# Attention head loop: the queries' cosine product on GpSimd instead of VectorE, and score tile 4 parted 320 + 320

## The reference

```python
q = jnp.einsum('bim,mhd->bhid', x, wq)          # 8 batches x 8 heads = 64 heads of 1024 x 128
k = jnp.einsum('bim,mhd->bhid', x, wk)
q = rope(q)                                     # [even*cos - odd*sin, even*sin + odd*cos]
k = rope(k)
s = jnp.einsum('bhid,bhjd->bhij', q, k) / D_HEAD
s = s - INFTY_APPROX * (i < j)                  # causal
p = jax.nn.softmax(s, axis=-1)
o = jnp.einsum('bhij,bhjd->bhid', p, v)
x = layernorm(x + jnp.einsum('bhid,hdm->bim', o, wo))
...                                             # then soft dispatch to 8 x 64 slots, gelu FFN, combine, layernorm
```

## Time and profile before

| | |
|---|---|
| time, three runs | 1764.21, 1767.45, 1772.24 us; median 1767.45 |
| the profiled execution | 1769.15 us, its span 1767.3 us |
| PE busy | 1694.9 us (96%) |
| DVE busy | 1431.5 us (81%) |
| ACT busy | 1237.6 us (70%) |
| POOL busy | 1134.0 us (64%) |
| q's cosine product on DVE (L616) | x64, 78.4 us, 1224 ns each |
| k's cosine product on POOL (L412) | x64, 153.0 us, 2390 ns each |

### The profile page before, as it was taken

How to read it: one execution, slowest core, us unless ns; L and a number is a source line. 1 busy time by engine, 2 the same in 40 slices (tenths; PEclk the granted TensorE clock), 3 DMA queues, 4 the chain that set the end, 5 groups by cost and what they waited for, 6 DMA issues and landing times. The chain is left out here.

```text
span 1767.3 us, 33370 instructions
## 1 busy us (share of the span) xinstructions
PE 1694.9 (96%) x10524; PEld 1481.7 (84%) x10524; DVE 1431.5 (81%) x2945; ACT 1237.6 (70%) x2361; POOL 1134.0 (64%) x684
## 2 busy tenths in 40 slices
PE   5999999999999999999999999999999997999996
PEld 4788888888888888888888888888888886889886
DVE  4888988897889888977898889879889887677764
ACT  3777777776777777767777777777777763665663
POOL 4566666665666656666666666666666654677775
PEclk9999999999999999999999999999999999999999
DMA  4222232223222322232223222322232323123212
GB/s 143 65 61 77 73 101 61 76 73 86 66 74 73 100 67 73 73 97 73 73 73 96 73 73 73 96 73 72 72 85 72 85 73 93 46 62 94 60 31 54
DMA packets 76518, 134.23 MB, mean 76 GB/s; under 512 B 19264, under 2 KB 45888, under 8 KB 76352
## 3 DMA queue, kind: packets, MB, share of 16 engines
q1 hardware_dynamic: 74880, 130.10, 27.7%
q10 hardware_dynamic: 1472, 2.10, 0.4%
HBM read 56.36 MB, written 8.70 MB: 37 GB/s over the span
## 5 line engine op out<-in xcount | busy, mean ns | idle before, releaser
L493 ACT ACTIVATE probs<-ps_slot,neg_max 128x640 f32<-128x640 f32 (+7 forms) x512 | 378.7, 741 | 121.1 <-DVE neg_max L600 111.7
L600 DVE CUSTOM_DVE_ANT_0 ps_slot<-ps_slot,causal 128x640 f32<-128x640 f32 (+7 forms) x512 | 386.8, 756 | 58.1 <-PE ps_slot L57 57.3
L816 PE MATMUL ps_turn<-ident,probs 128*128 128x128 f32 x2304 | 338.8, 277 | 19.8 <-DVE x_t L657 6.3
L426 POOL TENSOR_TENSOR q<-rot_q,q 128x1024 fp32r<-128x1024 f32 x64 | 153.9, 2404 | 245.0 <-ACT q L510 245.0
L816 PEld LDWEIGHTS ps_turn<-ident,probs 128*128 128x128 f32 x2304 | 257.7, 141 | 51.6 <-DVE x_t L657 8.0
L55 PE MATMUL ps_slot<-k,q 128*128 128x512 f32 (+3 forms) x768 | 285.0, 371 | 2.7 <-DVE rot_q L616 1.5
L57 PE MATMUL ps_slot<-k,q 128*128 128x512 f32 (+3 forms) x768 | 267.8, 349 | 0.0
L56 PE MATMUL ps_slot<-k,q 128*128 128x512 f32 (+3 forms) x768 | 267.1, 348 | 0.0
L418 POOL TENSOR_TENSOR swapped_q<-swapped_q,rope 128x1024 f32<-128x1024 f32 x64 | 170.8, 2669 | 77.0 <-DMA swapped_q<-unrot_q 76.9
L426 POOL TENSOR_TENSOR k<-rot_k,k 128x1024 fp32r<-128x1024 f32 x64 | 153.1, 2392 | 82.3 <-ACT k L510 79.8
L527 ACT ACTIVATE pt_split<-ps_turn 128x512 fp32r<-128x512 f32 x256 | 145.2, 595 | 61.8 <-PE ps_turn L816 61.8
(11 more groups left out here) (168 smaller groups left out, 4348.6 us busy)
## 6 DMA issues: line engine op xcount, KB each, us to landing
swapped_k<-unrot_k SPq DMA_DIRECT2D x128, 256.0 KB, 3.6
swapped_q<-unrot_q SPq DMA_DIRECT2D x128, 256.0 KB, 3.7
inv_b<-inv_rows SPq DMA_DIRECT2D x64, 512.0 KB, 5.0
x_rows<-in_L_attn_x SPq DMA_DIRECT2D x8, 512.0 KB, 5.2
y_t<-y_sum SPq DMA_DIRECT2D x8, 512.0 KB, 5.2
x_rows<-y_t SPq DMA_DIRECT2D x8, 512.0 KB, 3.9
unrot_q<-in_L_attn_x SPq DMA_DIRECT2D x8, 512.0 KB, 5.4
row_b<-r_rows SPq DMA_DIRECT2D x16, 256.0 KB, 3.5
```

Source lines behind the costliest of these rows:

```text
L426: pool.tensor_tensor(out[:, 1, :], rot[which][:, :], f32(out[:, 0, :]), ALU.subtract)\
L493: act.activation(probs_tile(t), score_tile(name, head, i), ACT.Exp, scale=-1.0, bias=neg_max[:, head.par, t:t + 1], accum_out=sums[:, head ...
L600: dve.tensor_tensor_reduce(tile, tile, causal[:, T - WIDTH[t]:T], -1.0, UNSEEN, ALU.add, ALU.min, neg_max[:, head.par, t:t + 1]).then_inc( ...
L816: last = pe.transpose(bank[:, at:at + P], probs_tile(t)[:, j * P:(j + 1) * P], ident[:, :])
```

## The change

The q cosine product leaves DVE's stream; POOL makes it, reading ACT's copy in SBUF, between its sine product for k and its sine product for q. With it the wait of PE before tile 7's scores changes from `cos_made[0]` to `raw_made[0]` (the copy), and SP waits for `cos_made[0]` once, near the end. The scores of tile 4 are placed 192 columns into their slot, so that the bank's border parts them into 320 and 320 columns. The first head is changed likewise.

```diff
+SLOT_OFFSET = {"s4": 192}
...
-            return slot(name, head)[:, i * BANK:i * BANK + WIDTH[t]]
+            at = i * BANK + SLOT_OFFSET.get(name, 0)
+            return slot(name, head)[:, at:at + WIDTH[t]]
...
-            def mul_cos_k(head):
+            def mul_cos(which, head):
                 if not head.live():
                     return
                 if head.step(-1).live():
-                    wait_apart(pool, lo_made[1], head.step(-1).made(), pool_ticks)
-                wait_apart(pool, raw_made[1], head.made(), pool_ticks)
-                pool.tensor_tensor(rot[1][:, :], unrot[1][:, :], kept.rope[:, 0, :], ALU.mult).then_inc(cos_made[1], 1)
+                    wait_apart(pool, lo_made[which], head.step(-1).made(), pool_ticks)
+                wait_apart(pool, raw_made[which], head.made(), pool_ticks)
+                pool.tensor_tensor(rot[which][:, :], unrot[which][:, :], kept.rope[:, 0, :], ALU.mult)\
+                    .then_inc(cos_made[which], 1)
...
                 before, after = head.step(-1), head.step(1)
-                mul_cos_k(after)
+                mul_cos(1, after)
                 mul_sin(1, after)
+                mul_cos(0, after)
                 mul_sin(0, after)
                 split_lo(1, after)
                 split_lo(0, after)
...
-            def mul_cos_q(head):
-                if not head.live():
-                    return
-                dve.wait_ge(raw_made[0], head.made())
-                if head.step(-1).live():
-                    dve.wait_ge(lo_made[0], head.step(-1).made())
-                dve.tensor_tensor(rot[0][:, :], slot("q", head), kept.rope[:, 0, :], ALU.mult).then_inc(cos_made[0], 1)
...
                 before, after = head.step(-1), head.step(1)
-                mul_cos_q(after)
                 invert(before)
...
-                    for c0 in range(0, WIDTH[t], BANK):
-                        cols = slice(c0, min(c0 + BANK, WIDTH[t]))
+                    room = BANK - SLOT_OFFSET.get(name, 0)
+                    for cols in (slice(0, min(room, WIDTH[t])), slice(room, WIDTH[t])):
+                        if cols.start >= cols.stop:
+                            continue
...
-                free_slot(cos_made[0], after)
+                free_slot(raw_made[0], after)
                 scores("s7", head)
```

More of the change, by code:

```diff
@@ L376, in step @@
                     sp.wait_ge(swap_landed[0], last * 32)
+                    sp.wait_ge(cos_made[0], last)
                     sp.dma_start(kept.x_row, x[0, :, :].rearrange("(t p) m -> p t m", p=P)).then_inc(ahead_landed, 16)
@@ L478, in _ @@
             pool.wait_ge(rope_landed, 32)
-            mul_cos_k(first)
+            mul_cos(1, first)
             mul_sin(1, first)
+            mul_cos(0, first)
             mul_sin(0, first)
@@ L754, in _ @@
             first = Head(0, 0, heads)
-            dve.wait_ge(rope_landed, 32)
-            mul_cos_q(first)
             dve.wait_ge(wvo_hi, 1)
@@ L873, in step @@
                 if head.live() and not before.live():
-                    pe.wait_ge(cos_made[0], head.made())
                     pe.wait_ge(raw_made[0], head.made())
```

## The result

The changed kernel takes **1785.27 us** (median of 6 runs, 1783.42 to 1786.93). The kernel before, run beside it, took 1767.45 (6 runs, 1764.21 to 1772.24). The ratio is 1.0096, with a 95% interval of 1.0079 to 1.0113: about one per cent slower. The forecast was 1785.0.

The account below looks back on a forecast made before the run. PE was taken to bound the kernel, level with DVE in heads with the long addition. Ordinary heads 4, other heads 3 and k's swap 10 made 17 us on 1769.15, 1.7 above the median: about 1785 us, range 1744 to 1804.

Parts of the forecast that it names:

- The shared pair and the chain: POOL instructions and DVE's two-SBUF-input additions exclude each other; sine k, cosine q, addition, sine q, low k, addition: 21.96 us a head.
- The hand-over between two POOL instructions: At k's addition, DVE gets SBUF access 0.14 us before POOL's recorded end, though POOL has its next instruction ready.
- The rival in which POOL isn't let go: POOL shuts DVE's addition for k out through q's cosine and sine products: 1.4 us more in 61 heads, near 1870; chance 0.13.
- L616 met nobody: DVE's old q cosine product, reading PSUM and SBUF, contended with no POOL instruction: its bare 1.22 us beside one.
- PE keeps the lead: Rival: DVE's addition for q precedes POOL's low part of k, or additions are hidden; 21.45 us a head, about 1743; chance 0.20.
- PE's 0.3 us buy nothing: PE's gain per head from tile 4's split and the removed tile 7 wait doesn't count, being outside the POOL-DVE sequence.
- The term of 4 + 3 us for ordinary and heavy heads: Attention loop: 52 ordinary heads lose 0.085 us each, 4 us; the nine others, six with the short addition, 3 us more.
- The term of 10 us for k's swap: q's swap, issued earlier, delays k's swap and POOL's sine product for k by x = 0.2 us in 52 heads.
- The rival with head 1's delay: k's swap late by 0.5 us or more: 1802, up to 1857 with head 1's 1.64; chance 0.07.
- The first head and the tail: POOL's added product in the first head, at most 2.4 us once, taken as 0; SP's added wait near the end stands behind finished work.

## Why the prediction was right, and where it was not

The time was right to 0.3 us. Taken apart, the mechanism holds, and one of its three terms doesn't.

- **The shared pair and the chain: right.** Start of the sine product of k to start of the sine product of q: 4.70 us (expected 4.72, from +2.98 to +7.70). Both additions in the long form in every head, 2.77 us (expected 2.8 and 2.7). The end of the chain leaves PE waiting for the low part of v, though by 0.39 us and not by 0.6 to 0.9: that sign was over-sized, and part of the delay shows as the wait for `pt_split`. An ordinary head takes 21.97 us (expected 21.96). The other sizes of the product show that its length enters the head one for one until PE leads.
- **The hand-over between two POOL instructions: right.** DVE gets the pair 0.14 us before POOL's recorded end in all 64 heads, for both additions (less 1.22 us from its end), and at the first of them POOL has the next instruction ready. The rival in which POOL isn't let go would have given 1870. The Trainium skill (SBUF — State Buffer, "SBUF: two separate sides") says that whichever of the two starts first gets the pair for its whole instruction and the other is blocked. The trace agrees: POOL's next is the one held out, 3.38 us in place of 2.39. That nothing is kept beyond one instruction was my reading of it, and the additions for k bear it out.
- **"L616 met nobody": right, by a weak proof.** In the row that I read, L616 had begun before POOL's product, so its bare 1.22 us proved nothing. The trace before has better: 15 of the 64 began inside a POOL instruction, and all 64 took 1.22 to 1.23 us.
- **"PE keeps the lead": refuted for the whole product, and real at three quarters.** I had priced it at 1743; the kernel with half a product takes 1743.5. The margin was what decided: 0.55 us less of POOL is worth 35 us.
- **"PE's 0.3 us buy nothing": right.** The changed kernel is as fast without the split. In the kernel before it buys nothing either, for another reason (the wait ahead of tile 7).
- **The term of 4 + 3 us for ordinary and heavy heads: too small.** From the first to the 63rd head the changed kernel needs 14.1 us more (1395.6 against 1381.5). 44 ordinary heads at 21.97 in place of 21.83 make 6; I had 0.085 a head, against a mean of before of 21.875. That mean was taken from L616 to L616; from one sine product of k to the next, as here, it is 0.05 less. The nine heavy heads went from 24.87 to 24.97, 1 us.
- **The term of 10 us for k's swap: wrong in its cause.** I took x = 0.2 in every head because q's swap is issued close behind k's. The step from the issue of k's swap to the sine product of k is 4.35 us at the median in both kernels: x is 0 in the ordinary head. What is there instead are nine heads with a mean of 22.70 (before: one of 22.52), some 7 us. In head 56 q's swap is issued 3.3 us behind k's in either kernel, and k's is late in both. The sine products of k around it, before and then after:

```profile
1247.63 2.39 POOL L418 TENSOR_TENSOR swapped_k<-swapped_k,rope 128x1024 f32<-128x1024 f32 x1 [0.46 <-DMA swapped_k<-unrot_k]
1270.15 2.41 POOL L418 TENSOR_TENSOR swapped_k<-swapped_k,rope 128x1024 f32<-128x1024 f32 x1 [1.18 <-DMA swapped_k<-unrot_k]
1291.43 2.40 POOL L418 TENSOR_TENSOR swapped_k<-swapped_k,rope 128x1024 f32<-128x1024 f32 x1 [0.44 <-DMA swapped_k<-unrot_k]
```

```profile
1261.96 2.40 POOL L422 TENSOR_TENSOR swapped_k<-swapped_k,rope 128x1024 f32<-128x1024 f32 x1 [0.44 <-DMA swapped_k<-unrot_k]
1284.77 2.41 POOL L422 TENSOR_TENSOR swapped_k<-swapped_k,rope 128x1024 f32<-128x1024 f32 x1 [1.32 <-DMA swapped_k<-unrot_k]
1306.70 2.40 POOL L422 TENSOR_TENSOR swapped_k<-swapped_k,rope 128x1024 f32<-128x1024 f32 x1 [0.45 <-DMA swapped_k<-unrot_k]
```

  Before, 22.52 us are followed by 21.28: the delay is caught up. After, 22.81 are followed by 21.93: it is lost. I had this half of the step ("each tenth there is a tenth of the period"), but what the change did was to use up the slack that had caught such delays, not to cause them. Why ten swaps were over 0.4 us late in this profile, against 2 before and 6 in each of two variants of the changed kernel, is open: with q's swap issued 1.9 or 3.9 us behind k's there were 6. The kernel before has 2 with the split as well, and 6 with the early reciprocal, so an earlier swap of q may have a part in it; these are counts of one profile each. (The rival with head 1's delay was also mis-summed: 52 heads of 1.64 us on 1775 give 1860, not 1857.)
- **The first head and the tail: taken as 0.** They have the rest of the 17.8 us between the two spans: 1.4 up to the sine product of k of head 1 (I had up to 2.4, and took 0), and 2.3 behind the 63rd head, whose cause I did not look for. These errors and the wrong term cancelled in the sum: 6 + 1 + 7 + 1.4 + 2.3 between the two profiled executions, where I had 4 + 3 + 10. The right total is partly luck.

## What to carry to other kernels

An engine that is idle a third of the time isn't free: where the instructions of two engines keep each other out, look at what the other is about to ask for in the very stretch into which the work goes. Instructions that hand over to each other like this make a chain, and how far it is from setting the pace (here half a microsecond of POOL) decides over the whole effect. Before moving work to take a wait away, look whether the work can be made earlier where it is; here one line in another order and a product in two halves, with the split, gave 20 us. A piece of work right ahead of a wait isn't worth speeding up until the wait is gone.

## What the runs showed that I had not expected

- The kernel before left it to 0.07 us whether a POOL instruction or the addition came first, and its two kinds of heads came of that. Starting POOL's instruction **earlier** (the sine product of q, by 0.9 us) made the time shorter by 7 to 8 us, though more of the additions for k were shut out (58 of 60 heads, before 28): the end of the exclusion counts, not its presence. That this is the whole gain is read from the trace; the reciprocal's earlier store moved with it.
- A late transfer costs next to nothing in a kernel that PE bounds and nearly its full length in one that is bound by a chain behind it: with half a product, head 56 has 21.98 and then 21.11 us, 0.13 more than two usual heads, for a delay of 0.45; in the changed kernel 22.81 and 21.93, 0.80 more, for a delay of 0.85.
- A POOL product has a fixed part: 1.30 us for 512 columns against 2.40 for 1024, so some 0.2 of it doesn't shrink.
